# Causal triangles in 64x64 quarters, the key mask as one row, and repeated products at the heads' beginnings

## The reference, cut to what matters

```python
# self attention
scores = jnp.einsum('bhqd,bhkd->bhqk', q, k) * SCALE
causal_bias = (1.0 - jnp.tril(jnp.ones((t, t), dtype=x.dtype))) * -10000.0
attn = jax.nn.softmax(scores + causal_bias, axis=-1)
out = jnp.einsum('bhqk,bhkd->bqhd', attn, v)
...
# cross attention over a context of 1601 keys; mask is (4, 1601), all ones here
Q = apply_rope((query @ Wq.T + bq) ..., cos_q, sin_q)
K = apply_rope((key @ Wk.T + bk) ..., cos_k, sin_k)
scores = jnp.einsum('bhqd,bhkd->bhqk', Q, K) * SCALE
scores = jnp.where(mask[:, None, None, :] == 0, neg_inf, scores)
attn = jax.nn.softmax(scores, axis=-1)
out = jnp.einsum('bhqk,bhkd->bhqd', attn, V)
```

## Time and profile before

| | us |
|---|---|
| median of 3 runs | 1852.01 |
| lowest, highest | 1838.22, 1853.08 |
| the profiled execution, its own time | 1846.2 |
| its span, first to last instruction | 1844.4 |
| TensorE busy | 1686.9 |
| VectorE busy | 1376.5 |
| ScalarE busy | 1052.5 |
| mean granted TensorE clock | 0.955 |

### The profile page before, as it was taken

The page is one execution under the profiler, slowest core; times in us unless marked ns, Lnnn a source line. Parts: engine busy times, 40 slices in busy tenths (PEclk is TensorE's granted clock), DMA queues, the critical chain, the costliest instruction groups (busy, mean ns, idle before and its releaser), DMA issues. The chain is left out here.

```text
span 1844.4 us, 34342 instructions
## 1 busy us (share of the span) xinstructions
PE 1686.9 (91%) x13310; PEld 916.1 (50%) x13310; DVE 1376.5 (75%) x2360; ACT 1052.5 (57%) x1764; POOL 686.6 (37%) x770
## 2 busy tenths in 40 slices
PE   8998999899999998889999887699999999999996
PEld 4886777668888885423332654122222222223564
DVE  4535888756676666778784788998999999994774
ACT  4322555345665563446666333177888888887552
POOL 2783777034544443413330343214412121111453
PEclk9999999999999999969999998599999999999998
DMA  6163999687876773601110586321201011000001
GB/s 219 54 214 137 308 322 326 221 308 290 312 294 265 293 296 129 178 11 35 28 36 2 179 227 191 63 64 43 82 20 37 19 28 29 19 20 1 24 12 35
DMA packets 114006, 247.62 MB, mean 134 GB/s; under 512 B 28154, under 2 KB 82974, under 8 KB 110240
## 3 DMA queue, kind: packets, MB, share of 16 engines
q1 hardware_dynamic: 87028, 207.68, 32.3%
q0 software_dynamic: 24176, 35.12, 7.3%
q10 hardware_dynamic: 2640, 2.62, 0.4%
HBM read 183.39 MB, written 61.38 MB: 133 GB/s over the span
## 5 line engine op out<-in xcount | busy, mean ns | idle before, releaser
L2198 DVE TENSOR_REDUCE Eh_maxima<-Eh_max 128x2 f32<-128x802 f32 x512 | 474.8, 987 | 25.1 <-PE Eh_max L2077 20.6
L2186 ACT ACTIVATE Eh_probs<-Eh_pair 128x1024 f32<-128x1024 f32 (+1 forms) x288 | 287.7, 999 | 112.7 <-PE Eh_pair L2116 112.7
L2077 PE MATMUL Eh_max<-Eh_KS,Eh_QS 49*128 49x401 f16 x1024 | 200.1, 360 | 44.8 <-DVE Eh_maxima L2198 40.9
L2139 PE MATMUL Eh_av_ps<-Eh_probs,E_V 128*17 128x512 f32 (+1 forms) x1664 | 225.5, 615 | 0.0
L1537 PE MATMUL C_y<-C_x_high,C_W 128*128 128x256 f16 (+1 forms) x1536 | 214.8, 253 | 9.5 <-ACT C_gate L1597 7.4
L2198 DVE TENSOR_REDUCE Dh_maxima<-Dh_max 128x2 f32<-128x1024 f32 x128 | 152.1, 1221 | 45.0 <-PE Dh_max L2085 43.0
L1537 PE MATMUL C_y<-C_x_low,C_W 128*128 128x256 f16 (+1 forms) x768 | 180.5, 252 | 0.0
L2186 ACT ACTIVATE Eh_probs<-Eh_single 128x512 f32<-128x512 f32 x272 | 161.5, 594 | 31.7 <-PE Eh_single L2116 31.6
L1915 POOL DMA_DIRECT2D Eh_KS<-E_kd x64 | 37.1, 580 | 355.3 <-PE Eh_pair L2116 350.1
L2077 PEld LDWEIGHTS Eh_max<-Eh_KS,Eh_QS 49*128 49x128 f16 x1024 | 50.9, 94 | 235.3 <-DVE Eh_maxima L2198 199.7
L1537 PEld LDWEIGHTS C_y<-C_x_high,C_W 128*128 128x128 f16 x1536 | 139.0, 98 | 22.9 <-ACT C_gate L1597 9.6
(11 more groups left out here) (457 smaller groups left out, 3527.0 us busy)
## 6 DMA issues: line engine op xcount, KB each, us to landing
C_W<-w_split SPq DMA_DIRECT2D x24, 3072.0 KB, 11.4
w_split<-B_w_parts SPq DMA_DIRECT2D x24, 768.0 KB, 9.8
Eh_KS<-E_kd POOLq DMA_DIRECT2D x64, 150.1 KB, 3.3
C_tail<-in_expert_tail_dram SPq DMA_DIRECT2D x24, 384.0 KB, 8.3
B_places<-in_w_experts_dram SPq DMA_DIRECT2D x10, 768.0 KB, 8.3
early_more<-in_w_experts_dram SPq DMA_DIRECT2D x8, 768.0 KB, 11.0
early_ctxT<-in_ctxT_dram SPq DMA_DIRECT2D x6, 800.5 KB, 5.9
early_ctxT<-in_w_experts_dram SPq DMA_DIRECT2D x6, 768.0 KB
```

Source lines behind the costliest of these rows:

```text
L2077: last = self.nc.tensor.matmul(bank[:, a, 0:self.cw], self.QS[r, slot, p, qt * P:(qt + 1) * P], self.KS[r, slot, p, k0:k0 + self.cw], star ...
L2139: last = self.nc.tensor.matmul(self.av_ps[u * STRIP:u * STRIP + VW, :], self.V[0:r, kt, unit * VW:(unit + 1) * VW], self.probs[0:r, self.b ...
L2186: self.nc.scalar.activation(dst, src, ACT.Exp, scale=1.0 / SCORE).then_inc(self.exp_done, 1)
L2198: self.nc.vector.tensor_reduce(self.maxima[:, g % 2, :, p * TPB + qt, c], self.max_ps[n % 2][:, :, 0:self.cw], AX_X, ALU.max).then_inc(sel ...
```

## The change

Three parts.

1. The self heads' mask: CAUSAL becomes S // HALF - 1 = 7 rows, for blocks of 64. What is left is two triangles of 64x64 for each block of 128. A new method `triangles` adds them with two 64x64 products for a unit, in the array's half a and in columns d * 64; two units fill the four quarters. 1024 of these stand in place of 512 products over the full array.
2. The cross keys' mask: no keep and no multiplication for keys. The mask row is made once for all four sequences on four partitions (is_equal 0, times -MASK), with the loads of a [128, 1601] mask for each sequence gone. The factor 64 goes into the rotary table (and out of the query's weights and bias). For a sequence whose mask is all zero, the queries are multiplied by zero: a flag for each sequence is spread over the partitions by a product with ones, and each query item is multiplied by it.
3. `keep_busy`: behind each maxima product before the first step one more product of the same operands for unit 0 alone, 256 columns for Dh and 384 for Eh, into `single_ps`, which nobody reads before the first scores write it.

```diff
-    def __init__(self, ctx, nc, name, n_keys, places, V, ATT, idents, tri, ahead, behind, order, start=None):
+    def __init__(self, ctx, nc, name, n_keys, places, V, ATT, idents, tri, ahead, behind, order, fill, start=None):
...
+    def keep_busy(self, m):
+        g, i, p, qt, c = self.max_parts(m)
+        slot, r = g % self.slots, slice(0, self.R)
+        self.nc.tensor.matmul(self.single_ps[:, 0:self.fill], self.QS[r, slot, p, qt * P:(qt + 1) * P], self.KS[r, slot, p, 0:self.fill],
+                              start=True, stop=True, tile_position=(0, 0))
...
-            last = self.nc.tensor.matmul(self.max_ps[n % 2][:, a, qt * P:(qt + 1) * P], self.ident_score[:], self.tri[:, 0, :], start=False, stop=True,
-                                         skip_group_check=True)
+            last = self.triangles(self.max_ps[n % 2][:, a, qt * P:(qt + 1) * P], a, 0)
         last.then_inc(self.filled, 1)
+
+    def triangles(self, block, a, side):
+        rows = slice(a * HALF, (a + 1) * HALF)
+        for d in range(2):
+            own = slice(d * HALF, (d + 1) * HALF)
+            last = self.nc.tensor.matmul(block[own, own], self.ident_score[rows, rows], self.tri[rows, side, rows], start=False, stop=True,
+                                         tile_position=(a * HALF, d * HALF), skip_group_check=True)
+        return last
...
+            if kind == "M" and m < self.n_max + self.ahead:
+                self.keep_busy(m)
...
-CAUSAL = TPB - 1
+CAUSAL = S // HALF - 1
...
-                load_mask(c)
+                if c == 0:
+                    sp.dma_start(mask[:], dram["mask"]).then_inc(mask_loaded, 16)
...
-                if n is not None:
-                    sp.wait_ge(row_ready, n + 1)
-                    sp.dma_start(mask_rows[b, :, :, c0:c0 + w], ...)
+                if p == 1:
+                    sp.wait_ge(row_ready, 1)
+                    sp.dma_start(mask_rows[:, 0], mask_row[:].rearrange("b (a w) -> b a w", a=1).broadcast_to([B, 2, S2])).then_inc(row_stored, 16)
...
+                    pe.wait_ge(each_ready, 1)
+                    pe.wait_ge(row_ones, 1)
+                    pe.wait_ge(after.copied_back, KD * B)
+                    mm(after.turn_ps[0][:, 0:B], ones[:], each[:], start=True, stop=True).then_inc(any_product, 1)
...
-                    row(n)
...
+            def mask_terms():
+                dve.wait_ge(mask_loaded, 16)
+                v.tensor_scalar(mask_row[:], mask[:], 0.0, -MASK, ALU.is_equal, ALU.mult).then_inc(row_ready, 1)
+                dve.wait_ge(row_ready, 1)
+                v.tensor_reduce(masked[:, 0:1], mask_row[:], AX_X, ALU.max).then_inc(count_ready, 1)
+                dve.wait_ge(count_ready, 1)
+                v.tensor_scalar(masked[:, 1:2], masked[:, 0:1], 0.0, None, ALU.is_equal).then_inc(flag_ready, 1)
+                dve.wait_ge(flag_ready, 1)
+                v.tensor_scalar(each[:], ident[0:B, 0:B], masked[:, 1:2], None, ALU.mult).then_inc(each_ready, 1)
...
                 if kn is None:
+                    if b == 0:
+                        dve.wait_ge(any_product, 1)
+                        v.tensor_copy(any_kept[:], after.turn_ps[0][:, 0:B]).then_inc(any_ready, 1)
+                        dve.wait_ge(any_ready, 1)
+                    v.tensor_scalar(t[:, n % 2, :, 0:w], t[:, n % 2, :, 0:w], any_kept[:, b:b + 1], None, ALU.mult).then_inc(kept, 1)
+                else:
                     dve.sem_inc(kept, 1)
-                else:
-                    v.tensor_tensor(t[:, n % 2, :, 0:w], t[:, n % 2, :, 0:w], keep[:, kn % 2:kn % 2 + 1, 0:w].broadcast_to([P, 2, w]),
-                                    ALU.mult).then_inc(kept, 1)
...
-                      ... "V M S S M V M S S M M S M S M S V M S M S V M S S M V S M S M S V R S M S M V S T", start)
+                      ... "V M S S M V M S S M M S M S M S V M S M S V M S S M V S M S M S V R S M S M V S T", 384, start)
```

More of the change, by code:

```diff
@@ L1865 @@
 SCORE = SCALE * SCALE
-MASK = 32768.0
+MASK = 16360.0
 UNITS = B * H
@@ L1920 @@
 class Heads:
-    def __init__(self, ctx, nc, name, n_keys, places, V, ATT, idents, tri, ahead, behind, order, start=None):
+    def __init__(self, ctx, nc, name, n_keys, places, V, ATT, idents, tri, ahead, behind, order, fill, start=None):
+        self.fill = fill
         self.nc, self.n_keys, self.causal, self.start = nc, n_keys, places.causal, start
@@ L2123, in bias_scores @@
         for i in range(first, first + w):
-            kt = i // STRIPS
-            last = self.nc.tensor.matmul(self.score_bank(i)[:, kt * P:(kt + 1) * P], self.ident_score[:], self.tri[:, 1, :], start=False, stop=True,
-                                         skip_group_check=True)
+            kt, u = divmod(i, STRIPS)
+            last = self.triangles(self.score_bank(i)[:, kt * P:(kt + 1) * P], u % 2, 1)
         last.then_inc(self.scored, 1)
@@ L2836, in phase_cross1 @@
     key_at = [p for p, (_, c) in enumerate(items) if c is not None]
[L2837 removed]
+    row_stored = ctx.enter_context(nc.semaphore("E_row_stored"))
+    stored = [[ctx.enter_context(nc.semaphore(f"E_{n}{i}")) for i in range(2)] for n in ("stored0_", "stored1_")]
     places = HeadPlaces(ctx, nc, "Eh", S2, 1, False, qd, kd, mask_rows, (dram["cross_k_rows"], dram["cross_q_rows"]), loaded, 1,
[L2839 removed]
+                        [(row_stored, 16)] + [(stored[i][m], 16 * (ITEMS // 2)) for i in range(2) for m in range(2)])
     tiles = [list(range(3 * c, 3 * c + 3)) for c in range(KC)]
@@ L2852, in phase_cross1 @@
         rotary = sb("rotary", [P, 4, S2])
-        mask = sb("mask", [P, S2], I32)
-        keep = sb("keep", [P, 2, CW], BF16)
+        mask = sb("mask", [B, S2], I32)
+        mask_row, masked, any_kept = sb("mask_row", [B, S2], F16), sb("masked", [B, 2]), sb("any_kept", [P, B])
+        each, ones = sb("each", [B, B]), sb("ones", [B, P])
         halves = sb("halves", [P, 2 * KD * S2], F16)
-        mask_row = sb("mask_row", [1, 2, CW], F16)
         t, other = sb("t", [P, 2, 2, S]), sb("other", [P, 2, S])
@@ L2997, in values @@
                     o.then_inc(v_copied, 1)
-            def row(n):
-                w = part_of(key_at[n])[3]
-                if n >= 2:
-                    act.wait_ge(row_stored[n % 2], 16 * (n // 2))
-                act.wait_ge(keep_ready, n + 1)
-                nc.scalar.activation(mask_row[:, n % 2, 0:w], keep[0:1, n % 2, 0:w], ACT.Copy, bias=-MASK, scale=MASK / SCALE).then_inc(row_ready, 1)
             def high(n):
@@ L3025, in first_scalar @@
                 n = part_of(p)[1]
-                if n is not None:
-                    row(n)
-                    if n >= 2:
-                        values(n)
+                if n is not None and n >= 2:
+                    values(n)
                 high(p)
@@ L3034, in first_gpsimd @@
             nc.gpsimd.memset(V[:].rearrange("p k (u v) -> p (k u) v", v=VW)[:, :, DH:VW], 1.0).then_inc(ones_ready, 1)
+            nc.gpsimd.memset(ones[:], 1.0).then_inc(row_ones, 1)
             for i, (signal, scale) in enumerate(((wk_loaded, E_WEIGHT), (wv_loaded, E_WEIGHT))):
@@ L3044, in first_gpsimd @@
             nc.gpsimd.tensor_scalar(wq[:].rearrange("p k e -> p (k e)"), wq[:].rearrange("p k e -> p (k e)"),
-                                    E_SCALE * E_QUERY, 0.0, ALU.mult, ALU.add).then_inc(w_scaled, 1)
+                                    E_SCALE * E_QUERY / SCALE, 0.0, ALU.mult, ALU.add).then_inc(w_scaled, 1)
             def lower(n):
@@ L3451, in lay_out @@
         "bv": columns(a["L1_xattn_bv"]), "bo": a["L1_xattn_bo"], "cross_WoT": a["L1_xattn_Wo"].T, "rotary": rotary,
-        "mask": np.repeat(a["mask_BxS2_if1"][:, None, :], P, axis=1),
+        "mask": a["mask_BxS2_if1"],
         "thKT": a["L0_attn_theta_K"].T, "thQT": a["L0_attn_theta_Q"].T, "thVT": a["L0_attn_theta_V"].T,
```

36 lines of the change are left out of this document (11 added, 25 removed).

## The result

| us | before | changed |
|---|---|---|
| median | 1846.24 (4 runs) | 1821.47 (4 runs) |
| lowest, highest | 1838.22, 1853.08 | 1820.40, 1822.59 |
| span of the profiled execution | 1844.4 | 1820.7 |

The ratio is 0.989 with a 95% interval of 0.9864 to 0.9915, so the changed kernel is about 1.1% faster. (The kernel before has a fourth run here, which moves its median.) Against the forecast of 1826.0 (1805 to 1854) the measured 1821.47 lies 4.5 us lower. In 40 further runs beside the experiments the kernel before had medians of 1842.35, 1839.98 and 1841.19 us.

What follows compares the result with a forecast made beforehand. TensorE was taken to bound the self heads at high clock, VectorE the cross heads, neither the key projections. Triangles 14, added products 0 and mask 8 sum to 22 us: 1824.2, plus 2 for the median, 1826 us (1805 to 1854).

Steps and rivals of the forecast that it cites:

- the mask's 8 us: Key projections: net saving from the mask row alone, limited by TensorE; 8 us, bounds 2 and 16.
- the 0.2 us given back a step: Self heads' step: 0.2 of the 1.09 us saved is lost to VectorE's late maxima where joined items follow each other.
- 14 us forecast: Self heads: triangles in quarters save 0.9 us net a step, 14 us in all.
- far end: Self heads: scores to quarters is no change of shape, the 0.2 us per group go too; 13 us more.
- the 7 us of rows 2: Self heads' beginning, 807.3 to 814.4 us: TensorE busy 6.96 of 7.10 us yet clock at 0.50; evidence against a lift.
- The clock's part: Key projections: stalls of 1 to 2 us instead of 3 save a third of some 5 us clock loss, 2 us.
- Cast waits for stores: Key projections: casts wait 8.6 us for stores of two-slot parts and reach that wait earlier, costing 2 us.
- expected relief of 13 to 15 us: Key projections: VectorE's net saving from dropped multiplications and keeps, less query multiplications and mask terms, 13 to 15 us.
- quarters in a row: Rival, self heads: quarters run one after another, each paying its start; 0 of the 14 us, 1840 us; chance 0.14.
- a lifted clock: Rival, beginnings of both heads' stages: added products lift the clock to 2.4 GHz, 9 us more, 1817 us; chance 0.18.
- free changes of shape: Rival, self heads: shape changes within half rows cost nothing, 13 us more, 1813 us; chance 0.08.
- the stuck clock: Rival, self heads: clock stays low beyond the first values, slower than before, 1880 us over eight steps; chance 0.14.

Runs made afterwards that it cites:

- half_array: The changed kernel with each triangle of 64 as a product in the scores' shape (64 rows, 128 columns of the array): 1809.3 us, ratio 0.9823.
- half_order: The changed kernel with triangles in the scores' shape, without the added products and with another order of letters in a self heads' step: 1798.26 us, ratio 0.9758.
- full_triangles: The changed kernel with its triangles put back over the full array (128x128, 3 causal rows), the other two parts kept: 1833.65 us, ratio 0.9947.
- multiply_kept: The changed kernel with one more VectorE operation, of the mask multiplication's length, in each of the 16 key items: 1832.47 us, ratio 0.9928.
- two_places: The changed kernel with both units' quarters in the first 64 rows of the array, two places instead of four: 1821.18 us, ratio 0.9888.
- double_quarters: The changed kernel with every quarter issued twice: 1828.34 us, ratio 0.9933.
- no_added: The changed kernel without the 52 added products at the heads' beginnings: 1816.79 us, ratio 0.9871; a second time 1818.44 us, ratio 0.9863.
- full_fill: The changed kernel with the added products as an identity over the full array, 128 rows by 128 columns: 1820.28 us, ratio 0.9884.

## Why the prediction was right, point by point

The time was within the range, the step of the self heads and the idle clock came as forecast, and the mask's route was right. Luck had a part: the mask's 8 us agree with the two profiles only by the dips, and the 0.2 us given back a step stand for another loss than the one named.

**Triangles: 14 us forecast, 14.1 measured in the stage, 12 by undoing them.** The forecast step was "about 12.3" and is 12.4 (in steady steps, which are free of the clock's changes). Two triangles' worth to the next product were to take 0.15 us and take 0.15 (902.60 to 902.75); four take 0.18 (907.86 to 908.04, the last three rows here) where full triangles took 0.33:

```profile
905.72 0.22 PE L2101 MATMUL Dh_pair<-carried_tri,D_ident_score 64*64 64x64 f16 x4
905.88 0.65 PE L2115 MATMUL Dh_max<-ident,Dh_av 128*128 128x128 f32 x4
...
907.86 0.22 PE L2101 MATMUL Dh_pair<-carried_tri,D_ident_score 64*64 64x64 f16 x4
907.91 0.20 PE L2101 MATMUL Dh_max<-carried_tri,D_ident_score 64*64 64x64 f16 x4
908.04 1.05 PE L2154 MATMUL Dh_av_ps<-Dh_probs,D_V 128*17 128x512 f32 x8
```

The gap ahead of the quarters stayed (902.28 to 902.60). By the rule of the Trainium skill (TensorEngine Tiling (Array Packing), Key Properties) a changed mode drains TensorE; the trace agrees, as the gap of 0.32 us stays with the quarters and is 0.22 in half_array, where the shape stays. That this is the price was the forecast's reason for not taking its far end.

One reason behind the number was wrong. I gave back 0.2 us a step to late maxima of VectorE. TensorE's busy time (162.36 of 162.80) leaves no room for such waits, so that the step came out as forecast is partly luck. What takes the 0.2 us are two places a step where two triangles save nothing, the turned token and the turned rows. Ahead of the token the full triangles were followed by a product of their own full shape, and quarters add a change of shape: the first two rows above have 0.16 us from four quarters to the token, where before two full triangles had 0.12, with no gap. Ahead of the turned rows it is 0.23 us (910.07 to 910.30) for 0.21 before. The sum had put 0.07 saved at each. The token before:

```profile
910.47 0.28 PE L2125 MATMUL Dh_pair<-carried_tri,D_ident_score 128*128 128x128 f16 x2
910.59 0.61 PE L2099 MATMUL Dh_max<-ident,Dh_av 128*128 128x128 f32 x4
```

**Added products: 0 forecast, nothing in the profiles, perhaps 3 us in the runs.** They fit beside VectorE's maxima as worked out (the maxima still come each 1.13 us in the self heads, 785.83 to 786.96, and each 0.90 in the cross heads, 1139.82 to 1140.72), and the clock did not follow, as the 7 us of rows 2 had let expect. In 12 of the 14 profiles the self heads' clock rises 1.8 to 3.5 us behind the first values. In half_order, whose order puts values earlier, it rises at 806.4 us after 27.3 us instead of 34 to 37 in those twelve, with TensorE busy for only 18.18 of them; its first values start at 807.5, so they are not what it waited for. What lifts it is not shown by these runs.

**Mask: 8 us forecast, 8.8 in the two profiles, 5.4 by undoing it, 4 to 5 with like dips.** The agreement of 8 and 8.8 is luck, since nearly half of the 8.8 is the dips. The route was right: TensorE's waits for V's copies, 10.6 us, were to shrink by six and shrank by 3.8, so they were not halved. The clock's part was called 2 us, for shorter stalls; in the profiles TensorE's busy time fell from 85.3 to 82.1 us for the same products, so 3.2, because both dips are absent. But with the new mask and two dips it is 85.2 (half_array) and 86.7 (full_triangles): shorter stalls do not keep dips away, and whether they make them rarer is not shown. Cast waits for stores were to cost 2 more. For the keys' store they are 8.6 us before and 7.9 after, but 4.9 to 15.2 over the eleven profiles without a multiplication of the keys, and one with 11.2 (and 6.2 for the queries' store) has the shortest projection, 96.2 us: they do not set the time there. Of VectorE's expected relief of 13 to 15 us only 9.3 came (91.87 to 82.6). The mask's terms and the four multiplications cost 6.7 us, 2 less than estimated; but the add ahead of the casts got longer, from 25.2 to 28.4 us in 20. (From 13.1 these two make 11.8; the other 2.5 us stand in no single row.) The reason stands in one timeline of the changed kernel:

```profile
1086.38 2.13 POOL L3059 TENSOR_TENSOR E_parts<-E_t,E_parts 128x1024 f16<-128x1024 f32 x1 [2.65 <-ACT E_parts L3022]
1087.28 2.04 DVE L3119 TENSOR_TENSOR E_t<-E_t,E_other 128x768 f32<-128x768 f32 x1
```

The add of 768 elements takes 0.96 us alone. Here it runs into GpSimd's subtraction for 1.23 us and takes 2.04, about as much more as the overlap. Summed over the 20 adds, the overlap grew from 5.9 to 8.9 us, and the adds by 3.2. It is not the missing multiplication that moved the adds on to GpSimd's time: with it put back (multiply_kept) they take 27.6 us with 8.7 of overlap, with the whole old mask 25.4 with 6.2. What of the old mask had held them off, a keep or a row of ScalarE, no run shows. The Trainium skill (SBUF — State Buffer, SBUF: two separate sides) has this as an exclusive lock on a shared port pair, held for the whole instruction; the trace agrees, nearly: the add is 1.08 us longer for 1.23 of overlap.

**The sum.** 22 us forecast, 23.7 between the profiles, of which 4.3 came with the dips that left the cross heads, some 4 with those that left the projection, and 3.5 were lost ahead of the self heads, none of it the change's as far as the runs show. By undoing part after part, 12 for the triangles, 5 for the mask and -3 to 0 for the products make 14 to 17; the ratio of 0.989 says 20 with 5 either way. So the gain was put a little too high, and the time still came out 4.5 us below the forecast, because of the base: the profile before was taken at 1846.2 us, and 2 us were added for a median of 1852.01 out of three runs, where the kernel's medians over 40 further runs are 1840 to 1842. The rivals: quarters in a row is refuted by two_places and double_quarters; a lifted clock by no_added and full_fill; free changes of shape by half_array and by the step of 12.4; the stuck clock did not occur in the two profiles of the changed kernel, but full_triangles shows a mild form, so that case is not excluded.

## What to carry to other kernels

Count changes of tile shape, not small products: where a small masking product can be given the shape of its neighbours, even if it then fills more of the array than it needs, the 0.1 us on both sides go, and here that was worth as much again as the quarters. When the bound has moved by that, look again at a hand-made order: the same order lost 0.2 us a step before and won 0.9 after. After taking work off one engine, look at what its remaining work now runs into. And before a difference of two profiles is called a gain, set it beside a profile with as much low clock in the same stage: here nearly half of the mask's 8.8 us was that.

## What the runs showed of the hardware that I had not expected

- Quarters in four places start on average 8 ns apart within a group (51 intervals a step, 0.40 us in all): 3 to 10 ns within a set of four, some 42 ns from one set to the next. The Trainium skill (TensorE: Matmul & The Clock Gate, "Wait — 56ns, not 53.3ns?") has about 25 ns as the least distance of two starts; this trace does not agree. It does not show that the distance holds for one place, either: in double_quarters, where each place gets two in a row, the records stand 6 to 7 ns apart.
- The clock stayed at 1.2 GHz with TensorE busy for 42.55 of 44.40 us on maxima and full-array products, and in full_triangles for 13.8 of 13.8 us with values among them, and rose in half_order after 27.3 us of which TensorE was busy for 18.18.
- Short dips to 0.50 in steady stretches of the cross heads stand behind the stretch of a step in which TensorE is busy least (2.31 of 3.4 us, in the mean 3.2), and those of the projection behind its longest waits (0.84 of 3.4). Equally thin stretches mostly pass without one, and which has one differs between runs of one kernel (the kernel before ranged from 1835.65 to 1853.08 us over all its runs). A dip of 3.4 us cost 1.4 us in the cross heads.
